# Two routed tiles a turn, with the last 48 hidden rows of both on the two row halves of the array

## The reference

```
x = x + xattn(layernorm(x), k, bias, ctx, ctx)       # a causal convolution over 256 places of products of x and ctx
x = x + ffn(layernorm(x))                            # a mixture of experts
  scores = softmax(xt @ Wg.T)                        # 2048 rows, 16 experts in 4 groups
  the 2 best groups, in them the 4 best experts of each row, weighted by their scores
  h = silu(xt @ W1[e].T) * (xt @ W3[e].T)            # 176 hidden numbers for each expert
  y = sum over the 4 experts of weight * (h @ W2[e].T)
  z = (silu(xt @ Ws1.T) * (xt @ Ws3.T)) @ Ws2.T      # shared experts, 352 hidden numbers
  out = y + z
```

## Time and profile before

| | |
|---|---|
| median of three runs | 396.6 us (396.31 to 396.92) |
| the profiled execution | 397.37 us |
| its span, first to last instruction | 395.6 us |
| TensorE matmul busy | 386.0 us, 98% of the span |
| TensorE weight load busy | 280.0 us, 71% |
| VectorE busy | 245.6 us, 62% |
| ScalarE, GpSimd busy | 161.0 us, 180.8 us |
| up of plain tiles (L1418) | 86.4 us in 256 records |
| down of plain tiles (L1492) | 66.2 us in 256 records |

### The profile page before, as it was taken

One profiled execution on the slowest core, in us unless ns is written; L12 is line 12 of the kernel. 1 busy time (PEld: TensorE's weight loads), 2 busy tenths in 40 slices (PEclk: granted clock), 3 DMA queues, 4 the chain that ended last, 5 costly groups with the idle time before them and its releaser, 6 DMA issues.

```text
span 395.6 us, 9072 instructions
## 1 busy us (share of the span) xinstructions
PE 386.0 (98%) x2146; PEld 280.0 (71%) x2147; DVE 245.6 (62%) x680; ACT 161.0 (41%) x487; POOL 180.8 (46%) x225
## 2 busy tenths in 40 slices
PE   7999999999999999999999999999999999999996
PEld 7888888888887646555666676446777777777775
DVE  3777577988987465788745344443446464646366
ACT  3347656565464363101124334333333333334441
POOL 3153323238888473555454333233334333335343
PEclk9999999999999999999999999999999999999999
DMA  8964573367878996256367973334474737372737
GB/s 246 372 247 141 171 273 138 136 204 286 310 248 319 416 420 261 92 193 228 104 203 230 318 247 107 86 93 141 124 242 140 244 110 239 113 245 88 269 95 261
DMA packets 37971, 83.09 MB, mean 210 GB/s; under 512 B 5962, under 2 KB 25902, under 8 KB 36016
## 3 DMA queue, kind: packets, MB, share of 16 engines
q1 hardware_dynamic: 31408, 64.83, 48.8%
q0 software_dynamic: 6528, 17.84, 11.6%
HBM read 60.21 MB, written 23.48 MB: 212 GB/s over the span
## 4 chain that ended last, share of the span: by engine, by line
PE 80%; DVE 9%; DMA 4%; issue 3%; ACT 2%; SPq 1%; DVEq 1%; POOL 0%; POOLq 0%
PE heads L1418 18%; PE bank L1492 13%; PE heads L1307 10%; PE heads L1460 9%; PE bank L1473 5%; PE heads L1309 5%; PE bank L1439 4%; PE heads L1428 4%; DVE kv L754 3%; PE bank L1321 3%; PE heads L1410 3%; PE bank L1484 2%; DMA ctx_rep<-ctxr_in 2%; DVE prod L785 2%; DMA y_scratch<-toep,dest_i 2%
## 5 line engine op out<-in xcount | busy, mean ns | idle before, releaser
L736 POOL DMA_INDIRECT y_scratch<-toep,dest_i x72 | 72.5, 1006 | 110.0 <-DVE dest_i L1164 93.1
L1418 PE MATMUL heads<-experts,toep 128*128 x256 | 86.4, 460 | 0.6 <-DVE toep L1122 0.5
L680 POOL DMA_INDIRECT rows_scratch<-rows,slot_i x64 | 63.2, 987 | 36.8 <-issue 18.9
L1307 PE MATMUL heads<-toep,kv 128*128 128x256 f32 x256 | 77.8, 386 | 2.2 <-DVE kv L754 1.5
L1492 PE MATMUL bank<-experts,toep 88*128 x256 | 66.2, 381 | 1.6 <-DVE toep L1129 1.6
L569 ACT ACTIVATE toep<-heads 128x176 f32<-128x176 f32 x72 | 22.9, 318 | 77.9 <-PE heads L1418 65.9
L1418 PEld LDWEIGHTS heads<-experts,toep 128*128 128x128 f32 x256 | 43.7, 190 | 14.7 <-issue 1.1
L1309 PEld LDWEIGHTS heads<-toep,kv 128*128 128x128 f32 x256 | 48.6, 190 | 6.6
L785 DVE TENSOR_TENSOR prod<-heads,ctx_rep 128x1024 f32<-128x1024 f32 x32 | 39.0, 1219 | 21.2 <-PE bank L1321 19.7
L1129 DVE COPY toep<-heads 88x256 f32<-88x256 f32 x72 | 30.2, 420 | 30.9 <-PE heads L1428 30.7
L1309 PE MATMUL heads<-toep,kv 128*128 128x128 f32 x256 | 49.2, 274 | 0.0
(11 more groups left out here) (245 smaller groups left out, 512.3 us busy)
## 6 DMA issues: line engine op xcount, KB each, us to landing
ctx_rep<-ctxr_in SPq DMA_DIRECT2D x15, 1024.0 KB, 4.9
experts<-experts_in SPq DMA_DIRECT2D x16, 608.0 KB
toep<-rows_scratch SPq DMA_DIRECT2D x56, 144.0 KB
prod<-y_scratch SPq DMA_DIRECT2D x5, 1024.0 KB, 5.5
rows_scratch<-pad_row SPq DMA_DIRECT2D x17, 144.0 KB, 1.8
ctx_tr<-ctxt_in SPq DMA_DIRECT2D x16, 128.0 KB, 4.7
toep<-toep_in SPq DMA_DIRECT2D x4, 512.0 KB, 8.1
ctx_n<-ctx_in SPq DMA_DIRECT2D x16, 128.0 KB, 2.0
```

The costliest lines, as they stand in the source:

```text
L680: pool.indirect_dma_start(rows_d, bass.IndirectOffsetOnAxis(ap=slot_i[:, u, k:k + 1].bitcast(U32), axis=0), rows[:, u, :], None).then_inc( ...
L736: pool.indirect_dma_start(y_d, bass.IndirectOffsetOnAxis(ap=dest_i[b][:, 0:1].bitcast(U32), axis=0), y_sb[b], None, bounds_check=TOPK * TO ...
L1307: nc.tensor.matmul(y_ps[par][:, i, :], kv[:, q, 0, h * P:(h + 1) * P], toep[:, k, :], start=True, stop=False)
L1418: last = nc.tensor.matmul(up_ps[p], x_tr[p][:, blk, :], up_w(e, blk), start=blk == 0, stop=blk == LB - 1)
```

## The change

Two tiles t and t+1 (t even) are now one turn on TensorE, VectorE and ScalarE.

- The 176 hidden numbers are split 128 + 48 instead of 88 + 88. Both tiles' last 48 stand beside each other in one block of 128 columns: columns 0 to 47 are the first tile's, 64 to 111 the second's, the rest zero. So `turn_h` is three transposes a pair (two blocks of 128, one block of both rests) instead of four, and `copy_h` one copy of 128 x 384 instead of two of 88 x 256.
- `down` begins with the rests: the first tile's 48 rows lie on partitions 0 to 47, the second's on 64 to 111. The two matmuls stand on the two row halves of the array, with the sums of the two tiles in two PSUM banks. Then come the two matmuls over 128 rows. The last 48 rows of W2 lie in the memory of the experts on both halves of the partitions; since one of them is read at a register's address, VectorE copies the second tile's 48 rows to a fixed place first (`rest_of_w2`). In mixed pairs the rests are four matmuls on the four quarters, then four on the column halves.
- VectorE takes both tiles' numbers first, then makes both hidden products (the second in two pieces, 48 and 128 columns), copies the weight rows, copies the transposed hidden numbers and places both destinations. The four sums of a read-back follow the pairs as one, two, one.
- TensorE's turn is turn_x(t+2), turn_x(t+3), down(t-2, t-1), turn_h(t, t+1), up(t+2), up(t+3): the hidden numbers of the pair in hand are transposed before the next pair's up.
- `WARM_UP` is 14 instead of 22.

SyncE's and GpSimd's orders are as before. The first fence shows a step of TensorE in the loop before, from `up` to the next tile's register load; L1418 is up, L1439 turn_x, L1492 down, L1428 turn_h.

Both takes now lie between the places of the old pair and the first product of the new one. The core of the diff:

```diff
-WARM_UP = 22
+WARM_UP = 14
...
-hid = [carve(INTER) for _ in range(2)]
-hid_tr = [carve(2 * P)[0:HI, :].rearrange("p (b n) -> p b n", b=2) for _ in range(2)]
+hid = carve(2 * P + HALF + REM)
+hid_main, hid_rest = (hid[:, 0:P], hid[:, HALF + P + REM:]), hid[:, P:2 * P]
+hid_tr = carve(3 * P).rearrange("p (c n) -> p c n", c=3)
+w2_rest = carve(L)
-ht_ps = [bank[i][0:HI, 0:2 * P].rearrange("p (b n) -> p b n", b=2) for i in (2, 3)]
+ht_ps = bank[2][:, 0:3 * P].rearrange("p (c n) -> p c n", c=3)
...
-def routed(eng, step, until):
-    for t in range(2 * DEPTH):
-        step(t, t % DEPTH, t // DEPTH)
-    for t in range(2 * DEPTH, until):
+def routed(step, until, eng):
+    for t in range(0, until, 2):
-        for b in range(DEPTH):
+        for b in range(0, DEPTH, 2):
-    for t in range(static, LIVE):
+    for t in range(static, LIVE, 2):
+def pair_of(t):
+    return t // 2
...
-def routed_step(t, b, before):
-    p = b % 2
-    silu(t, p)
-    if not (isinstance(t, int) and t == LIVE - 1):
-        src_tr(t + 1, 1 - p)
-    if not (isinstance(t, int) and t < 2):
-        store_y(t - 2, p, (b - 2) % DEPTH, before if b >= 2 else before - 1)
-routed(act, routed_step, 2 * DEPTH)
+src_tr(1, 1)
+def routed_pair(t, b, before):
+    silu(t, 0)
+    silu(t + 1, 1)
+    if not (isinstance(t, int) and t == LIVE - 2):
+        src_tr(t + 2, 0)
+        src_tr(t + 3, 1)
+    if not (isinstance(t, int) and t == 0):
+        for i in range(2):
+            store_y(t - 2 + i, i, (b - 2) % DEPTH + i, before if b >= 2 else before - 1)
+routed(routed_pair, 2 * DEPTH, act)
...
-        dve.wait_ge(ht_done, t - 1)
+        dve.wait_ge(ht_done, pair_of(t))
-    nc.vector.scalar_tensor_tensor(hid[p], act1[p], picked[:, b, 0:1], up_ps[p][:, INTER:],
-                                   ALU.mult, ALU.mult).then_inc(hid_ready, 1)
-def copy_h(w, p):
-    dve.wait_ge(ht_done, w + 1)
-    if not (isinstance(w, int) and w < 2):
-        dve.wait_ge(dn_done, w - 1)
-    nc.vector.tensor_copy(hid_tr[p], ht_ps[p]).then_inc(htr_ready, 1)
+    if p == 0:
+        nc.vector.scalar_tensor_tensor(hid[:, 0:INTER], act1[p], picked[:, b, 0:1], up_ps[p][:, INTER:],
+                                       ALU.mult, ALU.mult).then_inc(hid_ready, 1)
+    else:
+        nc.vector.scalar_tensor_tensor(hid_rest[:, HALF:HALF + REM], act1[p][:, P:], picked[:, b, 0:1],
+                                       up_ps[p][:, INTER + P:], ALU.mult, ALU.mult)
+        nc.vector.scalar_tensor_tensor(hid_main[p], act1[p][:, 0:P], picked[:, b, 0:1],
+                                       up_ps[p][:, INTER:INTER + P], ALU.mult, ALU.mult).then_inc(hid_ready, 1)
+def rest_of_w2(t, e, first):
+    if not (isinstance(t, int) and t < 2):
+        dve.wait_ge(rest_done, pair_of(t))
+    at = W13 + L
+    if first is not None:
+        nc.vector.tensor_copy(w2_rest[0:REM, :].unsqueeze(1), experts[0:REM, bass.ds(first, 1), at:at + L])
+    nc.vector.tensor_copy(w2_rest[HALF:HALF + REM, :].unsqueeze(1),
+                          experts[HALF:HALF + REM, bass.ds(e, 1), at:at + L]).then_inc(rest_ready, 1)
+def copy_h(m):
+    dve.wait_ge(ht_done, m + 1)
+    if not (isinstance(m, int) and m < 1):
+        dve.wait_ge(dn_done, 2 * m)
+    nc.vector.tensor_copy(hid_tr, ht_ps).then_inc(htr_ready, 1)
...
-def routed_step(t, b, before):
-    take(t, b, before)
-    hidden(t, b % 2, b)
-    if isinstance(t, int) and t < 2:
-        add_z(UNITS - 2 + t)
-    if not (isinstance(t, int) and t == 0):
-        copy_h(t - 1, 1 - b % 2)
+nc.vector.memset(hid_rest[:, REM:HALF], 0.0)
+def routed_pair(t, b, before):
+    first, e = take(t, b, before), take(t + 1, b + 1, before)
+    hidden(t, 0, b)
+    if isinstance(t, int) and t == 0:
+        add_z(UNITS - 2)
+    hidden(t + 1, 1, b + 1)
+    if isinstance(t, int) and t == 0:
+        add_z(UNITS - 1)
+    rest_of_w2(t, e, first if is_mixed(t) else None)
+    copy_h(pair_of(t))
     place(t, b, before)
+    place(t + 1, b + 1, before)
 def add_part(i, to, mem, step):
-        if pair is not None and 3 <= j <= 6:
-            add_pair(pair, u0, j - 3)
+        if pair is not None and j >= 2:
+            for step in ((0,), (1, 2), (3,))[j // 2 - 1]:
+                add_pair(pair, u0, step)
...
-def turn_h(w, p):
-    pe.wait_ge(hid_ready, w + 1)
-    if not (isinstance(w, int) and w < 2):
-        pe.wait_ge(htr_ready, w - 1)
-    for c in range(2):
-        last = nc.tensor.transpose(ht_ps[p][:, c, :], hid[p][:, c * HI:(c + 1) * HI], ident[:])
-    last.then_inc(ht_done, 1)
+def turn_h(t):
+    m = pair_of(t)
+    pe.wait_ge(hid_ready, t + 2)
+    if not (isinstance(t, int) and t < 2):
+        pe.wait_ge(htr_ready, m)
+    for p in range(2):
+        nc.tensor.transpose(ht_ps[:, p, :], hid_main[p], ident[:])
+    nc.tensor.transpose(ht_ps[:, 2, :], hid_rest, ident[:]).then_inc(ht_done, 1)
...
-def down(t, p, b):
-    e = pe.snap(expert_of[b], min_val=0, max_val=E - 1)
-    if not (isinstance(t, int) and t < 2):
-        pe.wait_ge(y_ready, t - 1)
-    pe.wait_ge(htr_ready, t + 1)
+def down(t, b):
+    e = [pe.snap(expert_of[b + i], min_val=0, max_val=E - 1) for i in range(2)]
+    if isinstance(t, int) and t < 2:
+        pe.wait_ge(z_added, UNITS)
+    else:
+        pe.wait_ge(y_ready, t)
+    m = pair_of(t)
+    pe.wait_ge(htr_ready, m + 1)
+    pe.wait_ge(rest_ready, m + 1)
+    lo, hi = slice(0, HALF), slice(HALF, P)
+    rest = [slice(0, REM), slice(HALF, HALF + REM)]
     if is_mixed(t):
-        for c in range(2):
-            nc.tensor.matmul(dn_ps[p][0:HALF], hid_tr[p][:, c, 0:HALF],
-                             down_w(e, c),
-                             start=c == 0, stop=c == 1)
-            last = nc.tensor.matmul(dn_ps[p][HALF:P], hid_tr[p][:, c, HALF:P], other_w2[t - MIXED0][:, c, :],
-                                    start=c == 0, stop=c == 1)
-        last.then_inc(dn_done, 1)
+        other = [other_w2[t - MIXED0 + i] for i in range(2)]
+        for half in (lo, hi):
+            for i in range(2):
+                w = w2_rest if half is lo else other[i][:, 1, :]
+                last = nc.tensor.matmul(dn_ps[i][half], hid_tr[rest[i], 2, half], w[rest[i], :],
+                                        start=True, stop=False)
+        last.then_inc(rest_done, 1)
+        for i in range(2):
+            nc.tensor.matmul(dn_ps[i][lo], hid_tr[:, i, lo], down_w(e[i]), start=False, stop=True)
+            nc.tensor.matmul(dn_ps[i][hi], hid_tr[:, i, hi], other[i][:, 0, :], start=False, stop=True
+                             ).then_inc(dn_done, 1)
-    for c in range(2):
-        last = nc.tensor.matmul(dn_ps[p], hid_tr[p][:, c, :],
-                                down_w(e, c),
-                                start=c == 0, stop=c == 1)
-    last.then_inc(dn_done, 1)
+    nc.tensor.matmul(dn_ps[0], hid_tr[rest[0], 2, :], rest_w(e[0]), start=True, stop=False)
+    nc.tensor.matmul(dn_ps[1], hid_tr[rest[1], 2, :], w2_rest[rest[1], :], start=True, stop=False
+                     ).then_inc(rest_done, 1)
+    for i in range(2):
+        nc.tensor.matmul(dn_ps[i], hid_tr[:, i, :], down_w(e[i]), start=False, stop=True).then_inc(dn_done, 1)
...
 turn_x(0, 0, 0, 0)
+turn_x(1, 1, 1, 0)
 down_shared(UNITS - 2)
-def routed_step(t, b, before):
-    p = b % 2
-    up(t, p, b)
-    if not (isinstance(t, int) and t == LIVE - 1):
-        turn_x(t + 1, 1 - p, (b + 1) % DEPTH, before + 1 if b == DEPTH - 1 else before)
+def routed_pair(t, b, before):
+    more = not (isinstance(t, int) and t == LIVE - 2)
+    if more:
+        for i in range(2):
+            turn_x(t + 2 + i, i, (b + 2) % DEPTH + i, before + 1 if b == DEPTH - 2 else before)
     if isinstance(t, int) and t == 0:
         down_shared(UNITS - 1)
-    elif not (isinstance(t, int) and t == 1):
-        if isinstance(t, int) and t < 4:
-            pe.wait_ge(z_added, UNITS - 3 + t)
-        down(t - 2, p, (b - 2) % DEPTH)
-    if not (isinstance(t, int) and t == 0):
-        turn_h(t - 1, 1 - p)
-routed(pe, routed_step, MIXED0 + MIXED + DEPTH)
-turn_h(LIVE - 1, (LIVE - 1) % 2)
-for t in range(LIVE - 2, LIVE):
-    down(t, t % 2, t % DEPTH)
+    else:
+        down(t - 2, (b - 2) % DEPTH)
+    turn_h(t)
+    if more:
+        for i in range(2):
+            up(t + 2 + i, i, (b + 2) % DEPTH + i)
+for i in range(2):
+    up(i, i, i)
+routed(routed_pair, MIXED0 + MIXED + DEPTH, pe)
+down(LIVE - 2, (LIVE - 2) % DEPTH)
 pe.wait_ge(xtr_ready, LIVE)
 for i in range(2):
     pe.wait_ge(last_in[2 * i], 16)
...
```

More of the change, by code:

```diff
@@ L42 @@
 INTER = 176
-HI = INTER // 2
+REM = INTER - P
 NSH = 2
@@ L182, in build @@
         other_w13 = [mem[:, 0:W13].rearrange("p (b n) -> p b n", b=LB) for mem in other_mem]
-        other_w2 = [mem[0:HI, W13:W13 + W2].rearrange("p (c n) -> p c n", c=2) for mem in other_mem]
+        other_w2 = [mem[:, W13:W13 + W2].rearrange("p (c n) -> p c n", c=2) for mem in other_mem]
         unit_sum = [bank[6 + i][:, 0:L] for i in range(2)]
@@ L228, in build @@
```

(35 more changed lines are left out.)

## The result

The changed kernel takes 405.7 us (median of 4 runs, 404.6 to 407.4), the kernel before 396.5 (4 runs, 396.1 to 396.9): a ratio of 1.0238, 95% interval 1.0217 to 1.0259. It is slower by 9.3 us; the forecast was 392.0 and its range ended at 400.5. The profiled execution took 407.4 (span 405.6, against 395.6 before).

The account below looks back on a forecast made before the run. TensorE's own instructions set the pace in the routed part. Gains of 7.7 + 3.9 + 1.3 = 12.9 us less 8.3 given back leave 4.6, so 396.6 becomes 392.0 us; range 386 to 400.5.

Parts of the forecast that it names:

- what is given back: Losses because pairing leaves less time between a free slot and TensorE wanting the next rows, and at the end: 8.3 us.
- Columns of a plain pair: TensorE's matmuls and transposes in a plain pair: 4.44 us instead of 4.98, with row halves side by side.
- rival D: Row halves run one behind the other, a plain pair is 5.18 us; 402.9 us in all, slower; chance 0.15.
- Changes of the array: Plain pairs change to row halves and back for 0.30 us, priced from column halves; 32 pairs give 7.7 us.
- Idle transposes: At the start, 14 instead of 22 idle transposes on TensorE win 1.3 us, bounds 0 and 1.45.
- Mixed pairs: Pairs with column halves: 5.19 us instead of 6.16, changes of the array five instead of eight; four give 3.9 us.
- Tiles 4 to 15: Crowded stretch: six pairs gain nothing (1.4 us lost), an expert load between a pair's gathers costs 1.5; together 2.9 us.
- rival C: Paired gathers come late everywhere, deciding from a landing of about 4.2 us; 400.4 us in all, slower; chance 0.20.
- which isn't in the sum: Possible price in the crowded stretch: after a long wait TensorE runs its records 0.216 us apart, as at the start.
- Read-backs and sums: Gathers behind each of four read-backs cost 0.6 us; two sums ahead of the takes cost 0.2 in each of five rounds.
- The end: TensorE's last down is longer by the rest (0.44 us) and the wider copy (0.13): 0.6 us.

Follow-up runs that it names:

- rest_twice: Changed kernel with the two matmuls over 48 rows of every plain pair done twice; 412.8 us, one run.
- before_loads: Kernel before with only the expert loads moved behind the gathers of tiles 9, 11, 13 and 15; 399.2 us, ratio 1.0043.
- best_22: Kernel best with 22 idle transposes instead of 14; 390.7 us, ratio 0.9835.
- before_14: Kernel before with 14 idle transposes instead of 22 and nothing else; 396.2 us, ratio 0.9982.
- short_sum: Changed kernel with the second of the two sums behind one pair adding 2 of 256 columns only; 408.9 us, ratio 1.0293.
- best: Changed kernel with the changes of early_take, order_only and loads_late, and one sum moved between hidden products and takes; 389.1 us, ratio 0.9805.
- loads_late: Changed kernel with the second to eighth expert load sent later, behind the gathers of tiles 9, 11, 13 and 15; 405.4 us, ratio 1.0199.
- order_only: Changed kernel with SyncE sending a round's fifth and sixth gather ahead of the store and read-back; 406.8 us, ratio 1.0263.
- loads_order: Changed kernel with both of SyncE's changes (order_only and loads_late), takes still behind the copy and casts; 406.8 us, ratio 1.0270.
- early_take: Changed kernel with the next pair's numbers taken right behind a pair's hidden products on VectorE; 402.2 us, ratio 1.0105.

## Why the prediction was wrong

The mechanism of the gain was right and the gaps were named at the right places; the sum of what is given back was far too small, because each place was priced alone, with nothing for what a late gather does to the next take, and nothing for the clock. Term by term, in us of the profiled executions (from the table of starts; minus is a gain):

| part | predicted | measured |
|---|---|---|
| start and first pairs, to tile 4 | -1.8 | -1.4 |
| tiles 4 to 14 | +1.7 | +5.6 |
| tiles 14 to 28, the mixed ones | -3.2 | -3.0 |
| tiles 28 to 70 | -1.6 | +6.9 |
| the end | +0.4 | +1.95 |

- *Columns of a plain pair*: right. The halves overlap, so rival D falls.
- *Changes of the array*: 0.39 a pair instead of 0.30. Column halves were the nearest row and not the same thing. 32 pairs give 4.9 instead of 7.7. What the Trainium skill says in "TensorEngine Tiling (Array Packing)", section Tiling Modes, that a change of mode drains the engine, agrees with this 0.39 for row halves. The Trainium skill's figure of 3.07 for four row tiles ("TensorE: Matmul & The Clock Gate", "Packing small matmuls") has no counterpart in two row halves: in rest_twice these keep full pace (0.22 and 0.21 apart); no run has four row tiles.
- *Idle transposes*: nothing shows of the 1.3, as its lower bound says. The text named the reason (another transfer becomes the last); the rows ended at 11.8 us, and the load that decides lands at 20. That the first line of the table fits is luck: at its first row transposes the changed kernel is 1.3 ahead of the kernel before (196.01 against 197.32), but so are before_loads (196.13) and best_22 (196.22) with 22 idle transposes, while before_14 (197.40) and short_sum (197.41) with 14 are not.
- *Mixed pairs*: right within 0.2, gains and late gathers together. An undisturbed mixed pair lasts 5.19 in best (244.99 to 250.18), the sum's number; in the kernel before six mixed steps lasted 18.31 (246.80 to 265.11), not 18.50, so two of them were 6.10.
- *Tiles 4 to 15*, the step that failed first: 2.9 was given for loads between the gathers. The mechanism was that one, since loads_late takes the loss at tile 8 away, and the landing of 4.82 is the case that rival C needed (from about 4.2). It stopped TensorE for 2.72 at tile 9, and then came the price "which isn't in the sum": 5 us at half the clock, 2.7 us. The text named this slower pace and gave it nothing; the same happened at the first read-back, where up lasted 3.47 instead of 2.37 at a mean granted clock of 0.68.
- *Read-backs and sums*, the step that failed worst: 0.6 and 0.2 a round, measured 0.8 and 0.8, and 3.6 at the first read-back. The takes were put at 0.65 each; behind another take one is mostly 0.83 to 1.04 in the changed kernel. So the hidden transposes do wait for VectorE, where the text expected almost none. The store's wait for the round's last sum, which now stands at the end of a pair and just ahead of the fifth gather, was overlooked: it is not in the list of what the change moves.
- *The end*: 1.95 instead of 0.4, and not on the path that was priced. The sum put it on TensorE's last down, which the chain of the kernel before runs through; the chain that ends the changed kernel runs through the last read-back (`394.42 7.35 DMA xn_tr_all<-y_scratch`) and VectorE's sums behind it. In best this read-back is waited for to 382.0; no experiment took it apart.
- *The rivals*: D's number (402.9) is the nearest, but its mechanism isn't there, so that is chance. Of the others C came nearest (400.4). Its condition, late everywhere, isn't met: plain turns without a load, sum or read-back are 4.83. But every tight place was late, and each by more than its own row said, since a late gather makes the take late, which makes the next gather late.

That last point is what the experiments show. Each mend alone (order_only, loads_late) and both together (loads_order) leave the ratio at 1.020 to 1.027, around the 1.024 of the changed kernel, though order_only and loads_late each take their own wait away: the wait moves on to the next link. Only early_take lengthens the time between asking and needing, and with it the same mends, with one sum moved, are worth some 12 us (ratio 1.0105 to 0.9805). The same turn of TensorE is thus 7.6 us under the kernel before with the requests made early, and 9.3 over it with VectorE and SyncE as the change left them.

## What to carry to other kernels

When work is paired or rotated, compute for each request how long before its use it is made, and move the request (here: the takes) by as much as the use moved; the slack of the old order is not a property of the new one. Late links in a ring of buffers (here four) don't add up one by one: a mend that shows its own wait gone and no time won has moved the wait, and the loop has to get slack as a whole. A matmul packed into half an array pays 0.2 us for each change of the array here, so look first at what else the packing saves.

## What was not expected of the hardware

- A change from the whole array to row halves or back costs 0.20 us here, to column halves or back 0.15; two row halves side by side run at full pace.
- After 2.7 us without work TensorE ran 5 us at a granted clock of 0.50; this wait cost as much again in clock.
- A gather of 144 KB sent among loads of 608 KB landed in 4.82 us, against a median of 2.7 for the late gathers before. By the Trainium skill, "DMA: Bandwidth & Descriptors", section "Queues, rings and completion order", each DMA engine consumes the descriptors of a ring in order. The trace agrees: the load that SyncE sent just ahead on its queue (213.39) took 5.6 us, to 219.0, and the gather landed 0.4 behind it.
- Two takes of VectorE in a row, each with a value loaded into a register, start mostly 0.83 to 1.04 us apart in the changed kernel, though the copy itself is 0.17; a shorter instruction ahead of them (0.16 instead of 0.69 us) didn't bring them forward.
